# Rotary angles in two pieces with per-octave turn tables, one table transfer a tile, and table rows fetched by indirect transfers

## What is computed

```python
pair = jnp.arange(0, DK, 2, dtype=jnp.float32)
inv_freq = 1.0 / 10000.0 ** (pair / DK)
omega_scale = jnp.exp(omega_log_scale)                       # (8 heads, 8 modes)
angles = pos[:, None, None, None] * omega_scale[None, :, :, None] * inv_freq
cos, sin = jnp.cos(angles), jnp.sin(angles)                  # 4096 x 64 x 32
qr = _l2norm(_rotary(q, cos, sin)) * scale
kr = _l2norm(_rotary(k, cos, sin))
...
def step(S, inp):                                            # 4096 steps, for each mode and head
    S = S * jnp.exp(b_g)[..., None, None]
    dv = (v_t[None] - einsum(k_t, S)) * b_beta[..., None]
    S = S + k_t[..., :, None] * dv[..., None, :]
    return (S, einsum(q_t, S))
```

## Time and profile before

| | before |
|---|---|
| median of 3 runs | 7800.08 us (7797.38 to 7800.09) |
| the profiled execution | 7801.93 us, of which its span is 7800.2 us |
| VectorE (DVE) busy | 6096.5 us, 78% |
| TensorE (PE) matmul busy, granted clock | 4588.7 us, 59%, 0.78 |
| ScalarE (ACT), GpSimd (POOL) busy | 3290.5 us, 3286.9 us, 42% each |
| DMA | 99.98 MB, 13 GB/s over the span |

### The profile page before, as it was taken

One profiled execution on the slowest core, in us unless ns is written; L12 is line 12 of the kernel. 1 busy time (PEld: TensorE's weight loads), 2 busy tenths in 40 slices (PEclk: granted clock), 3 DMA queues, 4 the chain that ended last, 5 costly groups with the idle time before them and its releaser, 6 DMA issues. The chain is left out here.

```text
span 7800.2 us, 198484 instructions
## 1 busy us (share of the span) xinstructions
PE 4588.7 (59%) x78633; PEld 3930.4 (50%) x78633; DVE 6096.5 (78%) x11133; ACT 3290.5 (42%) x5527; POOL 3286.9 (42%) x2021
## 2 busy tenths in 40 slices
PE   1565556655565555655556555665556555664994
PEld 0455445545455455554455454554555544554662
DVE  5788888888888888888888888888888888886003
ACT  0444444444444444444444444444444444443220
POOL 0544444444444444444443444444444444442003
PEclk6777778777777777877778777877777777887997
DMA  2000000000000000000000000000000000000223
GB/s 76 1 6 5 5 5 4 5 3 5 5 5 5 5 5 4 5 3 5 5 5 5 5 5 4 5 3 5 5 5 5 5 5 5 4 5 30 75 67 97
DMA packets 60165, 99.98 MB, mean 13 GB/s; under 512 B 11297, under 2 KB 48737, under 8 KB 58081
## 3 DMA queue, kind: packets, MB, share of 16 engines
q1 hardware_dynamic: 50784, 61.66, 2.4%
q0 software_dynamic: 8448, 25.18, 1.1%
HBM read 53.25 MB, written 33.55 MB: 11 GB/s over the span
## 5 line engine op out<-in xcount | busy, mean ns | idle before, releaser
L563 PE MATMUL bank<-rhs,te 128*64 128x64 f32 x8192 | 444.6, 267 | 1145.4 <-DVE rhs L1228 795.8
L1483 POOL TENSOR_TENSOR state<-state,gc_end 128x512 f32<-128x512 f32 x512 | 594.0, 1171 | 1122.4 <-PE bank L569 1066.3
L563 PEld LDWEIGHTS bank<-rhs,te 128*64 128x64 f32 x8192 | 371.6, 175 | 1231.1 <-DVE rhs L1228 1183.2
L546 PE MATMUL bank<-state,ke 128*64 128x64 f32 x16384 | 658.9, 248 | 349.9 <-DVE outT L1246 228.4
L546 PEld LDWEIGHTS bank<-state,ke 128*64 128x64 f32 x16384 | 617.4, 161 | 426.6 <-DVE state L1244 243.8
L737 ACT ACTIVATE te<-tt 32x256 f32<-32x256 f32 x1024 | 421.9, 412 | 896.2 <-DVE tt L1212 885.6
L1209 DVE TENSOR_TENSOR last_two<-last_two,prod 128x31 f32<-128x31 f32 (+15 forms) x1984 | 692.5, 349 | 68.1
L582 PE MATMUL last_two<-dvs,kte 128*64 128x64 f32 x16384 | 639.7, 236 | 172.2 <-DVE dvs L1235 172.2
L1207 DVE TENSOR_TENSOR prod<-bd,last_two 128x31 f32<-128x31 f32 (+15 forms) x1984 | 671.0, 338 | 71.7
L779 ACT ACTIVATE ke<-kq 32x512 f32<-32x512 f32 x1024 | 642.8, 628 | 198.3 <-DVE kq L1161 184.6
L582 PEld LDWEIGHTS last_two<-dvs,kte 128*64 128x64 f32 x16384 | 577.0, 150 | 188.2 <-DVE dvs L1235 179.2
(11 more groups left out here) (241 smaller groups left out, 11452.1 us busy)
## 6 DMA issues: line engine op xcount, KB each, us to landing
w_sb<-in_L_ffn_W_dram SPq DMA_DIRECT2D x16, 1024.0 KB, 9.3
expert_rows<-ke SPq DMA_DIRECT2D x1, 8192.0 KB, 21.0
xrows<-expert_rows SPq DMA_DIRECT2D x16, 512.0 KB, 8.3
expert_outputs<-yrow POOLq DMA_DIRECT2D x16, 512.0 KB, 3.4
xt<-_attn_hidden_states_dram SPq DMA_DIRECT2D x32, 128.0 KB, 2.1
xr<-_attn_hidden_states_dram SPq DMA_DIRECT2D x32, 128.0 KB, 2.0
x_after_attention<-xr SPq DMA_DIRECT2D x32, 128.0 KB, 1.7
xo<-x_after_attention SPq DMA_DIRECT2D x32, 128.0 KB, 3.7
```

The costliest lines, as they stand in the source:

```text
L546: mm = pe.matmul(bank_mem[g][s, q % 4 * DK:q % 4 * DK + DK], ke[:, c, r, q, s], state[:, hh * HQ + q, r, :], start=(r == 0), stop=(r == 1))
L563: pe.matmul(bank_mem[g][s, q % 4 * DK:q % 4 * DK + DK], te[:, q, s], rhs[:, q, :], start=True, stop=True)
L1483: pool.tensor_tensor(sv, sv, gc_end[:, vh, 4 * g:4 * g + 4, c].unsqueeze(2).broadcast_to([P, 4, 2 * DK]), ALU.mult).then_inc(sem(f"state_f ...
```

## The change

1. Angles in two pieces for all halves but the first two: the angle is split once, on the grid of `ROUND12`, and the third piece with its rounding and its subtraction goes. `angle_parts` has four operations in place of six; `turns_part` has two products and one sum in place of three and two. The two first halves (`general=True`) are computed in three pieces as before.
2. What makes two pieces enough are tables for the tile's octave (tile 1, tiles 2 and 3, 4 to 7, 8 to 15, 16 to 31), with the frequency scaled to match. For each octave five rows of 16 numbers (frequency and four table numbers) are put in `octave_tab`, stored to DRAM once for each tile of the octave (`turn_tables`), and SyncE loads the tile's own copy (128 x 80 numbers) into `tab` in each iteration, after `turns_summed` of the tile before. VectorE waits for `tab_in` ahead of its first use.
3. In the setup `look_up` over the exponents goes, and so does the load of the broadcast turn table. Instead VectorE makes row numbers, and GpSimd fetches 26 numbers (`TABS`) for each partition and quad with 16 indirect transfers; it waits for them ahead of its clearing. VectorE waits for them behind `setup_done`, packs `octave_tab`, and SyncE stores it with five transfers behind the load of the first tile. `octave_tab` lies in `qg`, so the first `queries_for_memories` waits for the stores.

```diff
-        turn = sb("turn", [P, 6, Q])
+        turn = sb("turn", [P, Q, TABS])
+        turn_row = sb("turn_row", [P, Q], U32)
+        tab = sb("tab", [P, 5, Q])
...
             sp.dma_start(xt[:], x2d[0:P, :]).then_inc(sem("x_in"), 16)
             load_again(0)
+            sp.wait_ge(sem("octaves_ready"), 1)
+            for o in range(OCTAVES):
+                sp.dma_start(tabs_dram[1 << o:2 << o].rearrange("n p x -> p n x"),
+                             octave_tab[:, o].rearrange("p k q -> p (k q)").unsqueeze(1).broadcast_to([P, 1 << o, 5 * Q])
+                             ).then_inc(sem("octaves_stored"), 16)
+            sp.wait_ge(sem("octaves_stored"), 16 * OCTAVES)
             with sp.Fori(1, NT) as n:
                 sp.wait_ge(sem("xn_ready"), since("xn_ready", n))
                 sp.dma_start(xt[:], x2d[bass.ds(n * P, P), :]).then_inc(sem("x_in"), 16)
+                sp.wait_ge(sem("turns_summed"), 2 * n)
+                sp.dma_start(tab[:].rearrange("p k q -> p (k q)"), tabs_dram[bass.ds(n, 1)].rearrange("a p x -> (a p) x")).then_inc(sem("tab_in"), 16)
                 store_sum(n - 1)
...
-            look_up(acc, turn_tab[:, 0], [turn_tab[:, 1 + i] for i in range(6)], [turn[:, i, :] for i in range(6)], NEXP)
+            lp(dve.tensor_copy(bh, acc.bitcast(U32)))
+            ts(bh, bh, 2.0 ** -23, None, ALU.mult)
+            vec(dve.tensor_copy(turn_row[:], bh), "turn_rows_ready", 1)
             lp(dve.reciprocal(er, acc))
             tt2(omega[:], omega[:], er, ALU.mult)
+            for o in range(OCTAVES):
+                ts(octave_tab[:, o, 0], omega[:], 2.0 ** (OCTAVES - 1 - o), None, ALU.mult)
...
             vec(dve.memset(state[:], 0.0), "setup_done", 1)
+            dve.wait_ge(sem("turn_in"), 16 * Q)
+            vec(dve.tensor_copy(octave_tab[:, :, 1:5, :], turn[:, :, 6:TABS].rearrange("p q (o k) -> p o k q", o=OCTAVES)), "octaves_ready", 1)
             dve.wait_ge(sem("cleared"), 1)
...
-            def angle_parts(n, hh, steps_):
-                om = omega[:, hh * HQ:hh * HQ + HQ].unsqueeze(2).broadcast_to([P, HQ, P])
+            def angle_parts(n, hh, steps_, general=False):
+                om = (omega[:] if general else tab[:, 0])[:, hh * HQ:hh * HQ + HQ].unsqueeze(2).broadcast_to([P, HQ, P])
+                grid = ROUND11 if general else ROUND12
                 for i in steps_:
                     if i == 0:
                         dve.wait_ge(sem("q_rotated"), since("q_rotated", 2 * n + hh))
+                        if not general:
+                            dve.wait_ge(sem("tab_in"), 16 * n)
                         ln(dve.tensor_tensor(tm[0], pos[:].unsqueeze(1).broadcast_to([P, HQ, P]), om, ALU.mult))
                     elif i == 1:
                         ln(dve.tensor_scalar(tm[0], tm[0], inv_freq, None, ALU.mult))
                     elif i == 2:
-                        ln(dve.tensor_scalar(tm[1], tm[0], ROUND11, -ROUND11, ALU.add, ALU.add))
-                    elif i == 3:
+                        ln(dve.tensor_scalar(tm[1], tm[0], grid, -grid, ALU.add, ALU.add))
+                    elif general:
                         ln(dve.tensor_tensor(tm[0], tm[0], tm[1], ALU.subtract))
-                    elif i == 4:
                         ln(dve.tensor_scalar(tm[2], tm[0], ROUND23, -ROUND23, ALU.add, ALU.add))
+                        vec(dve.tensor_tensor(tm[0], tm[0], tm[2], ALU.subtract), "parts_ready", 2 * n + hh + 1)
                     else:
-                        vec(dve.tensor_tensor(tm[0], tm[0], tm[2], ALU.subtract), "parts_ready", 2 * n + hh + 1)
+                        vec(dve.tensor_tensor(tm[0], tm[0], tm[1], ALU.subtract), "parts_ready", 2 * n + hh + 1)
...
                 if not last:
-                    angle_parts(n2, hh2, (2, 3))
+                    angle_parts(n2, hh2, (2, 3), general=first)
                 chunk_systems(u, 2)
-                if not last:
-                    angle_parts(n2, hh2, (4, 5))
                 chunk_systems(u, 3)
...
+            pool.wait_ge(sem("turn_rows_ready"), 1)
+            for q in range(Q):
+                pool.sem_inc(sem("pool_held"), 1)
+                pool.indirect_dma_start(out=turn[:, q, :], out_offset=None, in_=const_turn,
+                                        in_offset=bass.IndirectOffsetOnAxis(ap=turn_row[:, q:q + 1], axis=0)).then_inc(sem("turn_in"), 16)
+            pool.wait_ge(sem("turn_in"), 16 * Q)
             pool.wait_ge(sem("setup_done"), 1)
...
-            def turns_part(u, hh, first_table, into):
-
-                for i, part in enumerate((tm[1], tm[2], tm[0])):
-                    table = turn[:, first_table + 2 * i, hh * HQ:hh * HQ + HQ]
+            def turns_part(hh, general, low_part, into):
+
+                of = slice(hh * HQ, hh * HQ + HQ)
+                if general:
+                    pieces = [(part, turn[:, of, 2 * i + low_part]) for i, part in enumerate((tm[1], tm[2], tm[0]))]
+                else:
+                    pieces = [(part, tab[:, 1 + 2 * i + low_part, of]) for i, part in enumerate((tm[1], tm[0]))]
+                for i, (part, table) in enumerate(pieces):
                     ln(pool.tensor_tensor(low2 if i else into, part, over_t(table), ALU.mult))
-                    if i == 1:
+                    if i == 1 and general:
                         ln(pool.tensor_tensor(into, into, low2, ALU.add))
                 return pool.tensor_tensor(into, into, low2, ALU.add)
```

More of the change, by code:

```diff
@@ L39 @@
 NE2 = 65
-NEXP = 254
+OCTAVES = 5
+TABS = 6 + 4 * OCTAVES
 ROUND11 = 1.5 * 2.0 ** 12
+ROUND12 = 1.5 * 2.0 ** 11
 ROUND23 = 1.5
@@ L100, in shape_constants @@
     one = 1 << bits
-    rows = [[] for _ in range(7)]
+    turns = np.zeros((256, TABS), np.float64)
     for e in range(-126, 128):
[L103 to L110, removed]
+        row = []
+        for down, grids in [(0, (11, 23, 36))] + [(OCTAVES - 1 - o, (12, 24)) for o in range(OCTAVES)]:
+            for g in grids:
+                shift = e - down - g
+                v = inv2pi << shift if shift >= 0 else inv2pi >> -shift
+                v -= (v + one // 2) // one * one
+                hi = (v * 2048 + one // 2) // one
+                row += [hi / 2048 * 2.0 ** g, to_float(v - hi * one // 2048) * 2.0 ** g]
+        turns[e + 127] = row
+    turns = turns.astype(f)
     mat = np.concatenate([np.eye(P, dtype=f), neg, restart, of_mode, of_quad, before,
@@ L116, in shape_constants @@
                           (E * CAP + k[:, None] + T * np.arange(TOPK)[None, :]).astype(f)], 1)
-    return np.ascontiguousarray(mat), exps.reshape(1, -1), turns.reshape(1, -1)
+    return np.ascontiguousarray(mat), exps.reshape(1, -1), turns
 def build(nc, x_in, Wq, Wk, Wv, Wbeta, Wtg, mode_logits, log_decay, omega_log, Wg, Wo,
@@ L126, in build @@
     slots_dram = nc.dram_tensor("expert_rows", (2 * E * CAP, D), F32, kind="Internal").ap()
+    tabs_dram = nc.dram_tensor("turn_tables", (NT, P, 5 * Q), F32, kind="Internal").ap()
     y_dram = nc.dram_tensor("expert_outputs", (E * CAP, D), F32, kind="Internal").ap()
@@ L290, in build @@
         ld_col = tmp[:, 3, 8:9]
-        N_LOADS = 19
+        N_LOADS = 18
         ACT_TURNS = (12, 18)
         DVE_TURNS = (13, 28)
-        V_STEPS = (95, 220)
-        G_STEPS = (29, 34)
+        V_STEPS = (95, 216)
+        G_STEPS = (29, 26)
         def after(n, hh):
@@ L361, in _ @@
                      (exp_tab, const_exp.rearrange("a n -> (a n)").partition_broadcast(P)),
-                     (turn_tab.rearrange("p k e -> p (k e)"), const_turn.rearrange("a n -> (a n)").partition_broadcast(P)),
                      (wv_sb[:], Wv.rearrange("(k p) n -> p k n", p=P)),
@@ L1176, in turn_keys, with queries_for_memories @@
                 vec(dve.transpose(kt[:, 1], kq[:, 1, :, 0, :]), "kt_ready", u + 1)
-            def queries_for_memories(u):
+            def queries_for_memories(u, first):
                 dve.wait_ge(sem("q_rotated"), since("q_rotated", u + 1))
+                if first:
+                    dve.wait_ge(sem("octaves_stored"), 16 * OCTAVES)
                 for b4 in range(2):
@@ L1338, in half @@
                 chunk_systems(u, 0)
-                queries_for_memories(u)
+                queries_for_memories(u, first)
                 memories(update_memories, 3)
@@ L1343, in half @@
                 if not last:
-                    angle_parts(n2, hh2, (0, 1))
+                    angle_parts(n2, hh2, (0, 1), general=first)
                 chunk_systems(u, 1)
                 if not last:
-                    angle_parts(n2, hh2, (2, 3))
+                    angle_parts(n2, hh2, (2, 3), general=first)
                 chunk_systems(u, 2)
-                if not last:
-                    angle_parts(n2, hh2, (4, 5))
                 chunk_systems(u, 3)
@@ L1372, in _ @@
             weigh_decays(0)
-            angle_parts(0, 0, range(6))
+            angle_parts(0, 0, range(4), general=True)
             half(0, 0, first=True)
```

(23 more changed lines are left out.)

6 lines of the change are left out of this document (3 added, 3 removed).

## The result

| | before | after |
|---|---|---|
| median | 7798.73 us (7796.66 to 7800.09, 4 runs) | 7461.22 us (7459.73 to 7465.44, 4 runs) |
| ratio, 95% interval | | 0.9569 [0.9554, 0.9584] |
| profiled execution, span | 7801.93, 7800.2 us | 7465.44, 7463.6 us |
| first tile's statistics | 167.96 us | 111.24 us |
| a loop tile, mean of 30 (L1065 to L1065; L1085 to L1085) | 218.45 us | 209.46 us |

337 us faster, 5 us from the forecast of 7456. The setup gives 56.7 us and the loop 31 x 8.99 = 279.

The account below looks back on a forecast made before the run. The prediction took VectorE, busy 78% of the span, as the bound. Setup 57 plus loop 287 us (9.25 a tile, 31 iterations) made 344 off the profiled 7801.9, so 7458 and a median of 7456 us; range 7365 to 7545.

Parts of the forecast that it names:

- The bound, and where the gain would be: Loop: a chain of VectorE work, whose small operations are blocked while GpSimd works; 9.25 us a tile, 287 us.
- The pair in `hh` = 0: VectorE's removed L1100 and L1102, 1.99 us: the wait for TensorE's projection leaves 1.1 us; bounds 0.9 to 1.99.
- The pair in `hh` = 1, worth 0: Same two VectorE operations, 1.99 us: L1065's wait for ScalarE's root only grows to 4.2 us; bounds 0 and 1.99.
- The small operations of `hh` = 0: Both L1275 and L1277 on VectorE go free of GpSimd's shorter turns: 5.45 us a tile; bounds 3.7 and 7.0.
- The small operations of `hh` = 1: L1077 and L1078 go free, gain 2.97; L1071 and L1072 lose 0.3; net 2.7 us a tile, bounds 0.8 and 4.3.
- The table transfer: SyncE's load of 40 KB in each tile: cost 0, with 79 us of cover before its first reader.
- Rivals 1, 2, 3 and 5: 1: gains in full, 7367, 0.08; 2: blocking moves, 7709, 0.06; 3: plain count, 7620, 0.04; 5: three pieces remain, 7743, 0.01.
- The setup: Before the loop: look-up gone 57.5, small operations 1.6, load gone 2, loss 1; gain 57 us, bounds 46 and 60.
- the two paths: Setup, after row numbers at T: first tile at T + 36.7, GpSimd's gathers and clearing at T + 32.7, covered by 4 us.
- The 1 us that I took off: Setup: allowance for the last gathers queueing behind the 8 MB clearing; landing only with it would lose 10.3 us.
- the trap: Setup gathers: VectorE's two-port operations lock out GpSimd's descriptor writes; few stand beside them, time same within a microsecond or two.

Follow-up runs that it names:

- e1: Changed kernel with GpSimd's eight removed operations a tile put back as idle work, VectorE's left out: 7740.84 us, ratio 0.9924.
- e8: Kernel before with only `choose` moved, from step 12 to step 26 of the solve, nothing removed: 7591.69 us, ratio 0.9728.
- e2: Changed kernel with VectorE's two removed operations a half put back as idle work, GpSimd's turns still short: 7523.67 us, ratio 0.9648.
- e11: Changed kernel with `tile_norm` in the solve and `choose` at step 15 (7324 us), VectorE's two removed operations put back as idle work: 7425.64 us.
- e10: Changed kernel with the tile's tables fetched eight times, each transfer waiting for the last: 7455.74 us, ratio 0.956.
- e3: Kernel before with only `choose` moved, from step 12 to step 20 of the solve, nothing removed: 7689.91 us, ratio 0.986.
- e4: Kernel before with the new setup alone: three pieces everywhere, no octave tables or table transfers in the loop: 7750.23 us, ratio 0.9937.
- e5: Changed kernel with TensorE doing the product that sums the squares six times in place of once: 7465.22 us, ratio 0.9564.

## Why the prediction was right, point by point

**The bound, and where the gain would be: right.** That VectorE pays for GpSimd's turns was the step that carried the number. e1 and e8 show it from both sides.

**The pair in `hh` = 0: right.** 1.1 us forecast, 1.03 measured (1.99 less a wait that grows from 0.22 to 1.18 us). It is what the pair leaves at that wait; in e1 the same 1.03 went into longer waits for TensorE further on.

**The pair in `hh` = 1, worth 0: right as far as the wait goes** (2.22 to 4.21 us, and the waits in e2 and e11). By e2 the pair had a second effect, by shifting GpSimd's start in `hh` = 1, which the prediction used for phases but didn't add to the pair.

**The small operations of `hh` = 0: right.** 5.45 forecast, 5.44 measured (3.86 for the two L1275, 1.58 for L1277).

**The small operations of `hh` = 1: mechanism right, term mis-sized.** Forecast 2.7, measured 4.68: L1071 1.04, L1072 0.79, L1077 0.88, L1078 1.97. The prediction had L1072 held longer and a loss of 0.3 for L1071 and L1072 together. Its upper bound, 4.3 if both went free, was too low as well: at their quickest they take 0.22 and 0.28 us, so 2.97 and 1.8 make 4.8. It took ScalarE's copy (L761) to end 9.04 us behind L1065, as before. Now (L775, L1085) it ends 9.85 behind, GpSimd stands idle ahead of `squares` for 5.3 to 5.7 us and not for 4 to 5, `squares` begins at 4079.53, and VectorE's two operations at 4079.01 and 4079.27 slip in ahead of it:

```profile
4079.01 0.22 DVE L1091 COPY gb<-sg 64x128 f32<-64x128 f32 x1
4079.27 0.28 DVE L1092 TENSOR_SCALAR sg<-sg,rho 64x128 f32<-64x128 f32 x1
```
```profile
4079.53 1.04 POOL L1507 TENSOR_TENSOR rhs<-unit 128x512 f32<-128x512 f32 x1 [5.71 <-ACTq L776]
```

**TensorE's clock: not in the sum.** In a tile of 208.3 us the rows add up to 11.15 us and 10.1 are measured; the rest is waits for TensorE and GpSimd that grow by 0.15 to 0.37 us each in five places (1.4), less 0.3 that L1165's counterpart gives back. And 11 of 30 tiles take 3.1 us more, 1.1 a tile in the mean. Together they take back what `hh` = 1 gave too much: 8.99 a tile against 9.25. So the total is right to 5 us in part by luck: a term that was 2.0 us a tile too small, and 2.2 us a tile of waits that the sum put at nothing.

**The table transfer: right**, cost 0 (e10). **Rivals 1, 2, 3 and 5 are out**: the waits grew, the blocking ended, a plain count gives neither 279 us nor e1, and the loop has four operations.

**The setup: 57 forecast, 56.7 measured.** The row numbers are ready at 73.2 us (by the prediction's terms 74.72 - 2 + 0.6 = 73.3), the load is worth 2.2 us (2). Of the two paths the first tile's load decides, as the prediction said, and the other one, GpSimd's clearing, ends at 108.64, 2.6 us ahead of it:

```profile
93.01 0.95 POOL L1426 DMA_INDIRECT turn<-const_turn_dram,turn_row  x1 [0.30 <-issue]
99.71 1.80 POOL L1430 MEMSET kte<- 128x2048 f32 x1 [5.75 <-DMA turn<-const_turn_dram,turn_row]
```
```profile
111.24 0.43 DVE L1078 BATCH_NORM_STATS2 stat<-xt 128x6 f32<-128x256 f32 x1 [10.74 <-DMA xt<-_attn_hidden_states_dram]
```

The ten gathers issued ahead of the 8 MB clearing land 2.3 to 2.6 us behind the start of their issue, the six beside it 5.7 to 6.8. So the last one lands 5.75 us behind the end of its issue, where the sum had 3.5, and not with the clearing, which would have been some 18. The 1 us that I took off was lost on the other path: `setup_done` to the first tile's statistics takes 24.3 us in place of 23.3, and the clearing itself 21.9 in place of 21.0.

The Trainium skill ("SBUF — State Buffer", "SBUF: two separate sides") warns that GpSimd can't write descriptors while VectorE runs an operation in a two-port mode, such as an fp32 copy within SBUF. The gathers were issued every 1.25 us throughout. But such copies were few beside them, of 0.17 to 0.45 us, and the long operation there, of 6.9 us, is a memset and no copy; so the trap didn't show, and a long copy beside the gathers wasn't tried.

## What to carry to other kernels

When a small operation takes 2 us in one place and 0.2 in another, look at what GpSimd runs beside it: on VectorE's path that was worth 10.1 us a tile, where the removed instructions took 4.0 and gave 1.0. Moving small operations behind GpSimd's work gives such a gain with nothing removed, 6.8 us a tile in e8. Cost an operation at the next wait behind it, and where that wait swallows it, fill the wait instead: reordering alone took the changed kernel from 7461 to 7212 us. A phase is only good for the order in which it was read; every operation moved shifts those behind it against the other engine.

## What was not expected of the hardware

- A VectorE operation held by GpSimd ends at a fixed distance behind the end of the GpSimd operation, whichever that is: 0.02 us for 128x1, 0.03 for 128x8, 0.08 for 64x128 (L1071, L1072), 0.15 for the 128x256 of the norms, 0.28 for the scan (L1077), 0.55 for the 128x512 of L1078. It isn't slowed in proportion to its own length: 128x8 operations of 0.17 to 0.23 us took up to 2.39, and the CAST of e3, which met the end of a GpSimd operation, 0.78.
- The same loop can have two kinds of tile, 3.1 us apart, in an irregular order, with a granted TensorE clock of 0.94 and 0.82 in the same 28 us. In e4, whose loop has the instructions of the kernel before and starts 58 us earlier, there are four such tiles, where the kernel before has none (14 us in all). An earlier start alone isn't enough: e1 starts its loop 57 us earlier and has none.
- Making TensorE busier in one stretch raised its clock there from 0.50 to 0.99 and left the time as it was, within the interval (e5). What set the dips at the grams stays open.
